# An fp16-split FFN beside a sequential scan: the low part of the activated values is computed on GpSimd instead of VectorE

## Time and profile before

| | |
|---|---|
| median of 3 runs | 1740.26 us |
| profiled execution, its own time | 1741.27 us |
| span of its trace | 1739.5 us |
| busy: TensorE matmul / weight load | 1578.4 / 1362.0 us (91% / 78%) |
| busy: VectorE | 1542.2 us (89%) |
| busy: ScalarE | 785.7 us (45%) |
| busy: GpSimd | 48.3 us (3%), 36.1 of it in set-up |
| mean granted TensorE clock | 0.984 of full speed |

### The profile page before, as it was taken

One profiled execution on the slowest core, in us unless ns is written; L12 is line 12 of the kernel. 1 busy time (PEld: TensorE's weight loads), 2 busy tenths in 40 slices (PEclk: granted clock), 3 DMA queues, 4 the chain that ended last, 5 costly groups with the idle time before them and its releaser, 6 DMA issues.

```text
span 1739.5 us, 98588 instructions
## 1 busy us (share of the span) xinstructions
PE 1578.4 (91%) x39808; PEld 1362.0 (78%) x39808; DVE 1542.2 (89%) x11790; ACT 785.7 (45%) x5087; POOL 48.3 (3%) x49
## 2 busy tenths in 40 slices
PE   0067899999999999999999999899999999999997
PEld 0056788888888887888888888788878888788887
DVE  7978899999989998999989999899989999899992
ACT  3244444444444444444444444444444444444442
POOL 3400000000000000000000000000000000000000
PEclk9999999999989999999989999999999999999999
DMA  8400000000000000000000000000000000000000
GB/s 220 109 6 6 12 7 7 19 7 16 7 14 13 7 19 8 16 7 19 7 8 19 7 16 7 20 7 7 19 8 16 7 19 7 8 19 7 19 4 20
DMA packets 13591, 33.54 MB, mean 19 GB/s; under 512 B 1712, under 2 KB 6064, under 8 KB 12976
## 3 DMA queue, kind: packets, MB, share of 16 engines
q1 hardware_dynamic: 13104, 26.89, 5.8%
HBM read 22.69 MB, written 4.19 MB: 15 GB/s over the span
## 4 chain that ended last, share of the span: by engine, by line
PE 84%; DVE 6%; issue 2%; ACT 1%; DVEq 0%; POOL 0%; POOLq 0%; ACTq 0%
PE scan_ps L578 58%; PE gu_ps L316 18%; PE y_ps L330 8%; DVE q_stage L682 1%; ACT th L614 1%; DVE q_raw L682 1%; DVE with_p L647 1%; DVE th L653 1%; DVE with_q L647 1%; DVE q_sq L657 0%; DVE scan_ps L664 0%; DVE q_cub L660 0%; DVE xl L368 0%; DVE hist L772 0%; DVE p_part L647 0%
## 5 line engine op out<-in xcount | busy, mean ns | idle before, releaser
L578 PEld LDWEIGHTS scan_ps<-th,wscan 128*128 128x128 f16 x32768 | 988.6, 97 | 357.1 <-ACT th L614 252.3
L578 PE MATMUL scan_ps<-th,wscan 128*128 128x32 f16 (+1 forms) x32768 | 1119.8, 176 | 151.6 <-ACT th L614 123.8
L614 ACT ACTIVATE th<-q_stage 128x16 f16<-128x16 f32 x1536 | 318.7, 207 | 610.9 <-DVE q_stage L682 610.6
L316 PE MATMUL gu_ps<-xl,wffn 128*128 128x128 f16 x2816 | 394.8, 222 | 0.0
L316 PE MATMUL gu_ps<-xh,wffn 128*128 128x128 f16 x2816 | 393.3, 221 | 0.0
L653 DVE TENSOR_TENSOR th<-t,th 128x16 f16<-128x16 f32 x2048 | 348.7, 170 | 0.1
L616 ACT ACTIVATE t<-q_stage 128x16 f32<-128x16 f32 x1536 | 306.2, 199 | 0.0
L682 DVE TENSOR_REDUCE q_stage<-scan_ps 128x16 f32<-128x48 f32 x1536 | 256.6, 206 | 48.1 <-PE scan_ps L578 6.8
L316 PEld LDWEIGHTS gu_ps<-xl,wffn 128*128 128x128 f16 x2816 | 277.0, 98 | 0.3
L316 PEld LDWEIGHTS gu_ps<-xh,wffn 128*128 128x128 f16 x2816 | 267.0, 98 | 0.3
L614 ACT ACTIVATE th<-q_raw 128x16 f16<-128x16 f32 x512 | 105.9, 207 | 248.2 <-DVE q_raw L682 229.0
(11 more groups left out here) (40 smaller groups left out, 911.2 us busy)
## 6 DMA issues: line engine op xcount, KB each, us to landing
raw<-packed SPq DMA_DIRECT2D x11, 768.0 KB, 6.4
dr<-drive SPq DMA_DIRECT2D x34, 128.0 KB, 2.1
sc<-scales SPq DMA_DIRECT2D x11, 384.0 KB, 6.7
xres<-x SPq DMA_DIRECT2D x16, 256.0 KB, 3.5
out<-osb SPq DMA_DIRECT2D x16, 256.0 KB, 3.1
coup<-coupling_t SPq DMA_DIRECT2D x1, 1024.0 KB, 15.7
q_raw<-cond_t SPq DMA_DIRECT2D x1, 16.0 KB, 1.7
bias<-bias_t SPq DMA_DIRECT2D x1, 2.0 KB, 1.7
```

The costliest lines, as they stand in the source:

```text
L316: i = nc.tensor.matmul(gu_ps[b][:, half * P:(half + 1) * P], wffn[:, u, part, col:col + P], tokens[f.parity][:, kt, :], start=(r == 0), st ...
L578: i = nc.tensor.matmul(to if both else to[:, 0], wscan[:, w, part, kt, cols], moving if both else moving[:, 0], start=first, stop=last, sk ...
L614: nc.scalar.activation(th[s % 2][:, c, 0, :], q[:, c, :], ACT.Tanh, scale=1.0 / S).then_inc(now.tanh_hi, 1)
```

## The change

`ffn_hl` is issued on GpSimd by a new `pool_ffn`, in the place that the plan gives it in GpSimd's list, and no longer by `dve_ffn` on VectorE. It has the same operands and shape. It waits for `hh_ready` as before, and also for the down products of the unit that used the buffer before. `norm_root` moves into `pool_ffn`. The clearing of semaphores, which stood at the end of GpSimd's block, becomes a function called after stage 32's jobs, with the same waits. The tail's list on GpSimd takes the same form. The other engines' lists keep their order.

```diff
-        def ffn_hl(dve, f, u):
+        def ffn_hl(pool, f, g, u):
             b = (u + f.parity) % 2
-            dve.wait_ge(f.hh_ready, u + 1)
-            nc.vector.tensor_tensor(hl[b][:, :], h32[b][:, :], hh[b][:, :], ALU.subtract).then_inc(f.hl_ready, 1)
+            pool.wait_ge(f.hh_ready, u + 1)
+            wait_unit(pool, lambda s: s.down_done, f, g, u)
+            nc.gpsimd.tensor_tensor(hl[b][:, :], h32[b][:, :], hh[b][:, :], ALU.subtract).then_inc(f.hl_ready, 1)
@@ dve_ffn @@
-            if s in plan.hl:
-                ffn_hl(dve, f, plan.hl[s])
+        def pool_ffn(pool, plan, f, g, s):
+
+            if s in plan.hl:
+                ffn_hl(pool, f, g, plan.hl[s])
+            if s == plan.norm_root:
+                norm_root(pool, f)
@@ pool_block @@
+        def clear(pool, now, before, rest):
+
+            pool.wait_ge(now.clipped, HS)
+            pool.wait_ge(now.xres_in, 16)
+            pool.wait_ge(now.down_done, 2)
+            pool.wait_ge(now.drive_lo, 16)
+            if rest:
+                pool.wait_ge(before.out_ready, KT)
+            nc.gpsimd.sem_clear(before.range)
+            pool.sem_inc(now.other_cleared, 1)
+
         def pool_block(pool, now, before, ffn, rest):
             for s in range(STAGES):
-                for plan, f, _, at in jobs(now, before, ffn, rest, s):
-                    if at == plan.norm_root:
-                        norm_root(pool, f)
-            if before:
...
+                for job in jobs(now, before, ffn, rest, s):
+                    pool_ffn(pool, *job)
+                if s == 4 * HS and before:
+                    clear(pool, now, before, rest)
@@ pool_tail @@
-            norm_root(pool, before)
-            norm_root(pool, now)
+            for s in range(STAGES, SCHEDULE.end):
+                pool_ffn(pool, SCHEDULE, before, now, s)
+            for s in range(SCHEDULE.end):
+                pool_ffn(pool, SCHEDULE, now, before, s)
```

## The result

The changed kernel takes 1758.14 us (median of 4 runs, 1757.23 to 1759.2) and the kernel before 1740.2 beside it. The ratio is 1.0105, with a 95% interval of 1.0087 to 1.0122: slower by about 1%. The forecast was 1755.7, with a range of 1743 to 1790.

The account below looks back on a forecast made before the run. Each stage's first reduction sets the pace, held by VectorE's own work in stages like 8 and by products in stage 9. Held stages 14.9 plus tail 0.5 make 15.4 on 1740.3: 1755.7 us, range 1743 to 1790.

Parts of the forecast that it names:

- Nothing gained on VectorE: Scan stages with s = 1 modulo 4: removing 164 `hl` from VectorE gains 0, at most 1.6 us.
- The length of GpSimd's instruction: 128-column subtraction on GpSimd takes 0.43 us, between 0.26 and 0.81.
- When it starts: GpSimd starts `hl` 0.08 us after `hh` ends, so in stage 8 and no longer in stage 9.
- Who is held: VectorE's `with_q`, reading two SBUF tensors, waits for GpSimd's reading and ends 0.24 us later; the reduction comes 0.22 later.
- rival A: Whole scan: GpSimd's short instruction slips in between VectorE's, no cost and no gain, 1740.8 us; chance 11%.
- Which stages: Stages 4, 8, 12, 20, 24 pay 0.22 us each where held; stages 32, 36, 44, 48, 56, 60 pay 0.
- Rival B: Stages from 32 on pay too: reductions held, 11 us more, 1767, or `cube_in` held, 32 more, 1787; chance 13%.
- The even blocks' stage 4: Stage 4 of some even blocks waits for TensorE; 0.25 us spare covers the 0.22, so 4.4 units fall out.
- The tail: After the scan `hl` is 0.18 us later and TensorE waits for it three times: 0.5 us.
- The held stages: Stages below 32 where GpSimd's reading delays VectorE: 67.6 x 0.22 = 14.9 us.
- 2 us either way: Where the hardware loop jumps back, shorter VectorE code may move its stalls: an allowance of 2 us.

Follow-up runs that it names:

- no_hl: Low part `hl` left out on every engine, VectorE's list as in the changed kernel, down products using zeros: 1739.45 us, ratio 1.0003 to the kernel before.
- dummy_tt256: Kernel before, with an extra GpSimd subtraction of 256 columns on scratch tiles in the scan: 1775.16 us, one run.
- dummy_tt384: Kernel before, with an extra GpSimd subtraction of 384 columns on scratch tiles in the scan: 1820.06 us, one run.
- dummy_memset: Kernel before, with an extra GpSimd memset of 384 float32 columns, which reads nothing: 1739.4 us, ratio 1.0001.
- dummy_tt128: Kernel before, `hl` still on VectorE, with GpSimd's 128-column subtraction added into a scratch tile in the scan: 1754.92 us, ratio 1.0087.
- late_hh: Changed kernel, with ScalarE's drive sums moved to even stages so `hh` ends 0.24 us later in stages 4 to 24: 1743.48 us, ratio 1.0025 to the kernel before.
- delay_pool: Changed kernel, with a 64-column GpSimd memset and a wait ahead of `hl` for units 0 to 3 and 10: 1744.13 us, ratio 1.0027 to the kernel before.
- keep_count: Changed kernel, with VectorE keeping one instruction, a wait raising an unread semaphore, in place of each `hl`: 1757.89 us, ratio 1.0104 to the kernel before.

## Why the prediction was right

**Nothing gained on VectorE.** The equal lengths of stages 9 and 29 said so, and no_hl showed it directly.

**The length of GpSimd's instruction.** 0.43 from a slope and a one-column row, 0.428 measured. Of the two one-column rows the 0.19 was the right one; dummy_tt256 and dummy_tt384 confirm the line.

**When it starts.** 0.08 after `hh`, in the stage of `hh` and not of the old `hl`. Measured 0.078.

**Who is held.** That a VectorE instruction held by GpSimd ends at GpSimd's end plus its own length minus 0.14 came from a 1536-column pair in set-up, and it held for 32 columns: `with_q` 0.42 against a forecast of 0.43, the stage 0.215 against 0.22. So rival A fell: a short instruction does not slip in between. That GpSimd has to read was behind the step, and dummy_memset against dummy_tt128 shows it. I had put the hold down to VectorE's two SBUF inputs. Two kinds of instruction passed untouched: the reductions from PSUM in dummy_tt384, and in late_hh the 14 `osb` instructions (L390, one input in PSUM and one in SBUF) that start 0.04 after GpSimd's and still take 0.34. But two SBUF inputs are not the whole condition, and set-up of the kernel before had shown it. This is VectorE's second unpacking step, which shifts and masks the one tensor `nib` in SBUF, and then GpSimd:

```profile
15.95 3.73 DVE L520 TENSOR_SCALAR nib<-nib 128x1536 int32<-128x1536 int32 x1
...
15.63 3.23 POOL L471 TENSOR_TENSOR wffn<-w,wffn 128x1536 f16<-128x1536 f32 x1 [14.64 <-ACT wffn L483]
```

It takes 0.96 with GpSimd idle. Here it ends at 19.68, 0.82 after GpSimd, again its own length minus 0.14. So an instruction with one SBUF input can be held as well; which of them are, no run here sorts out. The forecast did not need it, as the local terms of a stage have two.

**Which stages.** The five below 32 and not the six from 32 on. late_hh and delay_pool, two ways of one shift, took 14 of the 18 us away, so the place in the stage is what decides. Here the prediction was too smooth: it gave the second half zero, which is right for an undisturbed stage, but the lead is so small that a VectorE stall of 0.1 us in stage 44 turns it over. In the changed kernel itself the stalls happened to sit elsewhere. That is luck: at the places that they have in the kernel before, these seven stages cost 1.8 us more, as dummy_tt128 and keep_count show. Rival B was the right fear, in 7 stages of 90 and in other kernels than this.

**The even blocks' stage 4.** TensorE covered it: in blocks 4, 6, 8 and 10 it is not longer (-0.01 to -0.04), in block 12 by 0.12 and in block 14 by 0.22.

**The tail.** 0.5 forecast, 0.56 measured. TensorE waits for `hl` three times, as before, a little longer each:

```profile
PEld y_ps L330 <- POOL hl L360: 3.9, 3, 1.7
```

**The rest of the sum.** The forecast of 15.4 falls 2.5 short of the 17.9 between the medians. Of that 1.7 lies between the medians and the traces, whose spans differ by 16.2: the profiled execution of before was 1.1 above its median, that of after 0.5 below. The held stages came out as forecast (14.5 for 14.9), in part because +0.7 and -0.8 from other causes cancel in them. In the trace the term that it had only as "2 us either way" is +1.7 (the sum of -0.7, +0.9 and +1.5). That term holds both the moved stalls and the first two stages of the blocks, where the loop jumps back, which alone are +1.5; the traces of one execution each don't tell how much of that is chance.

## What to carry to other kernels

Before an elementwise instruction goes from VectorE to GpSimd, look for what VectorE does at the moment at which GpSimd will run it, and not at the moment at which it stood in VectorE's list: if a VectorE instruction with two SBUF inputs is due then, and sets the pace, it waits until GpSimd has read. A VectorE instruction with one SBUF input can be held too, as `nib` was. An engine that is 89% busy may still have free time exactly where the instruction stood; two stages of one kind, with it and without it, tell that from the trace of before. If the work must go over, a delay of a few tenths of a microsecond into a stretch in which VectorE reads PSUM takes most of the cost away, 14 of 18 us here. It did not make the move pay: the instruction had cost nothing on VectorE, and both shifted kernels stayed about 0.3% above the kernel before.

## What the runs showed of the hardware

- GpSimd's subtraction of float32 minus fp16 into fp16 on 128 partitions took 0.428, 0.670, 0.913 and 3.09 us for 128, 256, 384 and 1536 columns. A memset of float32 took 0.151 for 64 and 0.418 for 384 columns, a copy to fp16 0.294 for 128.
- Who goes first is not fully explained by "asks 0.13 after its start". In stage 8 of the even blocks VectorE is late, GpSimd's instruction is the long one of 0.62, and the held one is `cube_in`. Block 8, VectorE and GpSimd:

```profile
916.10 0.18 DVE L666 SCALAR_TENSOR_TENSOR q_cub<-q_sq,hist 128x32 f32<-128x32 f32 x1
916.20 0.18 DVE L653 SCALAR_TENSOR_TENSOR with_q<-hist,with_p 128x32 f32<-128x32 f32 x1
916.32 0.41 DVE L670 SCALAR_TENSOR_TENSOR scan_ps<-q_cub,with_p 128x32 f32<-128x32 f32 x1
...
916.05 0.62 POOL L360 TENSOR_TENSOR hl<-h,hh 128x128 f16<-128x128 f32 x1 [0.56 <-ACT hh L354]
```

  GpSimd started 0.05 ahead of `q_cub` and 0.15 ahead of `with_q`, and both went first. In block 9 it started 0.06 ahead of `with_q` and went first itself. The cost was the same, one hold, but the rule for the order stays open.
- VectorE's list has stalls, each worth 0.07 to 0.35 us of a stage's length, whose places move when instructions are taken out of the list, and go back when the count is restored (keep_count). The Trainium skill, "Advanced Engine Details and Errata", section "ISA Cache", gives a cache line of 256 instructions; that these stalls are such lines no run here shows.
